# A graph attention layer on one core: the factor of neighbour j moves from h into the weights, the mask becomes a minimum, and h is split in chunk 0 by ScalarE and VectorE

## What is computed

```
h  = relu(layernorm(x)) @ W1 + b1                      # 4096 x 256
e  = leaky_relu((h @ a1)[:, None] + (h @ a2)[None, :] + b2, 0.2)
attention = softmax(where(adj > 0, e, -1e12), axis=1)  # row i over neighbours j
out = x + elu(attention @ h)
```

## Time and profile before

| what | value |
|---|---|
| median of 3 runs | 459.96 us |
| lowest and highest run | 459.87, 460.02 us |
| span of the profiled execution | 458.2 us (its own time isn't shown) |
| median less span | 1.76 us |
| busy share of the span: TensorE, VectorE, ScalarE, POOL | 93%, 85%, 67%, 28% |
| mean granted TensorE clock | 0.989 |
| DMA | 80.60 MB, mean 176 GB/s |

### The profile page before, as it was taken

The page is one execution under the profiler, slowest core; times in us unless marked ns, Lnnn a source line. Parts: engine busy times, 40 slices in busy tenths (PEclk is TensorE's granted clock), DMA queues, the critical chain, the costliest instruction groups (busy, mean ns, idle before and its releaser), DMA issues.

```text
span 458.2 us, 8873 instructions
## 1 busy us (share of the span) xinstructions
PE 423.9 (93%) x3399; PEld 416.1 (91%) x3399; DVE 387.6 (85%) x388; ACT 309.1 (67%) x297; POOL 126.3 (28%) x155
## 2 busy tenths in 40 slices
PE   0799879788889999999999999999999999999995
PEld 0789879787888899999999999999999999999995
DVE  3999799999998805999999549999996399999915
ACT  2687898777665418995776289958663789586603
POOL 3242289999999940000000000000000000000004
PEclk9999998989899999999999999999999999999999
DMA  8930025554543630754738806656468156566202
GB/s 279 382 132 1 1 92 185 183 185 185 183 176 109 240 118 14 263 199 169 255 158 285 292 21 226 232 183 224 188 237 295 63 191 259 192 208 250 92 0 92
DMA packets 22355, 80.60 MB, mean 176 GB/s; under 512 B 1472, under 2 KB 14016, under 8 KB 14144
## 3 DMA queue, kind: packets, MB, share of 16 engines
q1 hardware_dynamic: 21920, 79.70, 49.0%
q10 hardware_dynamic: 416, 0.66, 0.4%
HBM read 76.15 MB, written 4.19 MB: 175 GB/s over the span
## 4 chain that ended last, share of the span: by engine, by line
PE 67%; POOL 12%; issue 9%; DVE 7%; DMA 2%; POOLq 1%; ACT 1%; SPq 0%; DVEq 0%; ACTq 0%
PE ps L599 39%; PE ps L601 19%; POOL h_raw L325 12%; DVE stats L656 2%; DMA x_s<-x 2%; PE ps L617 1%; PE ps L616 1%; PE ps L615 1%; DVE hnT_lo L683 1%; PE ps L526 1%; DVE h_raw L692 1%; PE ps L528 1%; PE ps L527 1%; DVE y L868 1%; DVE xn L673 1%
## 5 line engine op out<-in xcount | busy, mean ns | idle before, releaser
L599 PE MATMUL ps<-hp_hi,w_hi 128*128 (+1 forms) x960 | 240.5, 288 | 12.7 <-POOL hp_lo L328 12.5
L601 PE MATMUL ps<-hp_lo,w_hi 128*128 (+1 forms) x960 | 238.1, 285 | 0.0
L730 DVE SCALAR_TENSOR_TENSOR adj_s<-R,p,adj_s 128x1024 f32<-128x1024 f32 x128 | 171.7, 1382 | 38.8 <-ACT adj_s L392 38.8
L599 PEld LDWEIGHTS ps<-hp_hi,w_hi 128*128 128x128 f32 x960 | 184.5, 192 | 17.4 <-issue 12.7
L601 PEld LDWEIGHTS ps<-hp_lo,w_hi 128*128 128x128 f32 x960 | 184.4, 192 | 0.0
L400 ACT ACTIVATE w_hi<-adj_s 128x2048 fp32r<-128x2048 f32 x64 | 122.5, 1913 | 56.0 <-DVE adj_s L730 38.5
L740 DVE SCALAR_TENSOR_TENSOR w_lo<-adj_s,w_hi 128x2048 fp32r<-128x2048 f32 x64 | 153.1, 2394 | 3.7 <-ACT w_hi L400 3.7
L392 ACT ACTIVATE adj_s<-adj_s 128x2048 f32<-128x2048 int32 x64 | 122.2, 1910 | 20.1 <-DMA adj_s<-adj_t 20.1
L599 PE MATMUL ps<-hp_hi,w_lo 128*128 (+1 forms) x960 | 125.2, 283 | 0.6 <-DVE w_lo L740 0.6
L599 PEld LDWEIGHTS ps<-hp_hi,w_lo 128*128 128x128 f32 x960 | 119.5, 189 | 0.8 <-DVE w_lo L740 0.8
L339 POOL TENSOR_TENSOR adj_s<-y,adj_s 128x256 f32<-128x256 f32 x8 | 5.7, 712 | 283.8 <-DVE y L868 283.5
(11 more groups left out here) (88 smaller groups left out, 269.1 us busy)
## 6 DMA issues: line engine op xcount, KB each, us to landing
adj_s<-adj_t SPq DMA_DIRECT2D x64, 1024.0 KB, 4.8
x_s<-x SPq DMA_DIRECT2D x8, 512.0 KB, 10.4
o_s<-x SPq DMA_DIRECT2D x3, 1024.0 KB, 8.5
out<-o_s SPq DMA_DIRECT2D x6, 512.0 KB, 6.9
adj_s<-x SPq DMA_DIRECT2D x1, 1024.0 KB, 5.5
out<-adj_s SPq DMA_DIRECT2D x8, 128.0 KB, 1.7
vec<-vectors ACTq DMA_DIRECT2D x1, 384.5 KB, 6.4
W1x<-W ACTq DMA_DIRECT2D x1, 256.0 KB, 4.4
```

The source lines that it names most:

```text
L599: last = pe.matmul(acc, block_w, hh, start=False, stop=False)
L601: pe.matmul(acc, block_w, hl, start=False, stop=False)
L730: last = dve.scalar_tensor_tensor(sgn, R[:, ds(ic * CW, CW)], p[:, ds(source(r, c) + s, 1)], sgn, ALU.max, ALU.mult)
```

## The change

The factor u_j is taken out of h and put into the weight:

- `sign` (the name stays) is a Relu with the factor 2^102, so that it gives 0 or a very large number; the mask is a minimum with it.
- `high` is a copy with the factor u of each tile, so two instructions of 1024 columns in place of one of 2048; `low` likewise is two instructions, weight times u less `w_hi`. `high` of the first pair leaves group 7 and comes in its place in the loop, after u.
- `hp_hi` is now the rounded h (`round_h`, a pair in one instruction), and `hp_lo` is h less `hp_hi` (`low_h`, a pair in one instruction on VectorE). POOL's loop is gone.
- TensorE waits for `hp_ready` once a pair, and multiplies with 256 columns of `hp_lo`, since the low part of the columns 1 and 0 is zero. The other matmuls keep 258.

```diff
+BIG = 2.0 ** 102
@@ gpsimd
-            def hp_low(jb):
-                rows = h_raw[:, ds(jb, 1), :]
-                pool.wait_ge(hp_tile, jb + 1)
-                pool.tensor_tensor(rows, rows, u[:, ds(jb, 1)].unsqueeze(2).broadcast_to([P, 1, HW]), ALU.mult)\
-                    .then_inc(hp_whole, 1)
-                pool.wait_ge(hp_whole, jb - 1)
-                pool.tensor_tensor(hp_lo[:, ds(jb, 1), :], rows, hp_hi[:, ds(jb, 1), :].bitcast(fp32), ALU.subtract)\
-                    .then_inc(hp_ready, 1)
-            with pool.Fori(2, TILES) as jb:
-                hp_low(jb)
@@ scalar
-                act.activation(adj_w[:, c, :, :], adj_s[:, c, :, :], ACT.Sign).then_inc(signed, 1)
+                act.activation(adj_w[:, c, :, :], adj_s[:, c, :, :], ACT.Relu, scale=BIG).then_inc(signed, 1)
...
-                act.activation(w_hi[:, c, :, :], adj_w[:, c, :, :], ACT.Relu).then_inc(hi_ready, 1)
+                for s in range(2):
+                    last = act.activation(w_hi[:, c, s, :], adj_w[:, c, s, :], ACT.Copy, scale=u[:, ds(source(r, c) + s, 1)])
+                last.then_inc(hi_ready, 1)
...
-                if g == 7:
-                    high(0, 0, 0)
...
+            def round_h(r, c):
+                pair = ds(source(r, c), 2)
+                act.activation(hp_hi[:, pair, :], h_raw[:, pair, :], ACT.Copy).then_inc(hp_pair, 1)
+            act.wait_ge(ones_col, 1)
+            round_h(0, 0)
             act.wait_ge(g_ready, 1)
             act.activation(u[:, :], s2[:, :], ACT.Exp, bias=gm[:, 4:5]).then_inc(u_ready, 1)
-            def hp_high(r, c):
-                for s in range(2):
-                    jb = source(r, c) + s
-                    act.activation(hp_hi[:, ds(jb, 1), :], h_raw[:, ds(jb, 1), :], ACT.Copy,
-                                   scale=u[:, ds(jb, 1)]).then_inc(hp_tile, 1)
@@ scalar, round_of
-                        hp_high(*ahead(ic, r, c, 1)[1:])
+                        round_h(*ahead(ic, r, c, 1)[1:])
...
-                    if not (first and r is FIRST_ROUND and c == 0):
-                        high(ic, r, c)
+                    high(ic, r, c)
...
-            act.wait_ge(ones_col, 1)
             act.wait_ge(u_ready, 1)
-            hp_high(0, 0)
             keep_s(GROUPS - 2)
@@ tensor, pair
-                        if first and part == 0:
-                            if begin:
-                                pe.wait_ge(hp_first, s + 1)
-                            else:
-                                pe.wait_ge(hp_ready, 2 * m + s - 1)
+                        if first and part == 0 and s == 0:
+                            pe.wait_ge(hp_ready, m + 1)
...
-                        hl = hp_lo[:, ds(2 * m + s, 1), :]
+                        hl = hp_lo[:, ds(2 * m + s, 1), 0:F]
...
-                                pe.matmul(acc, block_w, hl, start=False, stop=False)
+                                pe.matmul(ps[:, ib, 0:F].unsqueeze(1), block_w, hl, start=False, stop=False)
@@ vector
-                                                    ALU.max, ALU.mult)
+                                                    ALU.max, ALU.min)
...
-                dve.scalar_tensor_tensor(w_lo[:, c, :, :], adj_w[:, c, :, :], 0.0, w_hi[:, c, :, :].bitcast(fp32),
-                                         ALU.max, ALU.subtract).then_inc(lo_ready, 1)
+                for s in range(2):
+                    last = dve.scalar_tensor_tensor(w_lo[:, c, s, :], adj_w[:, c, s, :], u[:, ds(source(r, c) + s, 1)],
+                                                    w_hi[:, c, s, :].bitcast(fp32), ALU.mult, ALU.subtract)
+                last.then_inc(lo_ready, 1)
...
+            def low_h(r, c):
+                pair = ds(source(r, c), 2)
+                dve.wait_ge(hp_pair, pair_no(0, r, c) + 1)
+                dve.tensor_tensor(hp_lo[:, pair, :], h_raw[:, pair, :], hp_hi[:, pair, :].bitcast(fp32), ALU.subtract)\
+                    .then_inc(hp_ready, 1)
@@ vector, round_of
                     low(ic, r, c)
+                    if first and not (r is LAST_ROUND and c == SLOTS - 1):
+                        low_h(*ahead(ic, r, c, 1)[1:])
...
-            for jb in range(2):
-                dve.wait_ge(hp_tile, jb + 1)
-                dve.scalar_tensor_tensor(hp_lo[:, jb, :], h_raw[:, jb, :], u[:, jb:jb + 1], hp_hi[:, jb, :].bitcast(fp32),
-                                         ALU.mult, ALU.subtract).then_inc(hp_first, 1)
+            low_h(0, 0)
             dve.wait_ge(p_ready, 2)
+            dve.wait_ge(u_ready, 1)
```

More of the change, by code:

```diff
@@ L197, in build @@
         eps_ready = sem("eps_ready")
-        hp_tile = sem("hp_tile")
         dve_y = sem("dve_y")
         dve_o = sem("dve_o")
-        hp_first = sem("hp_first")
-        hp_whole = sem("hp_whole")
+        hp_pair = sem("hp_pair")
         hp_ready = sem("hp_ready")
@@ L607, in last_pair @@
                 if first:
-                    pe.wait_ge(hp_ready, 2 * m)
+                    pe.wait_ge(hp_ready, m + 1)
                 for ib in range(BANKS):
@@ L613, in last_pair @@
                         hh = hp_hi[:, ds(2 * m + s, 1), :]
-                        hl = hp_lo[:, ds(2 * m + s, 1), :]
+                        hl = hp_lo[:, ds(2 * m + s, 1), 0:F]
                         pe.matmul(acc, w_hi[:, b, s, col], hh, start=False, stop=False)
-                        pe.matmul(acc, w_hi[:, b, s, col], hl, start=False, stop=False)
+                        pe.matmul(ps[:, ib, 0:F].unsqueeze(1), w_hi[:, b, s, col], hl, start=False, stop=False)
                         last = pe.matmul(acc, w_lo[:, b, s, col], hh, start=False, stop=s == 1)
```

## The result

The changed kernel takes **440.53 us** (median of 4 runs, 439.96 to 440.69), the kernel before 459.91 beside it (459.67 to 460.02). The ratio is 0.9578, 95% interval 0.9565 to 0.9592: faster by 4.2%. The forecast was 440.5. The profiled execution is the fastest of the four: 439.96 us at a span of 438.2; the spans of the four are 438.2, 438.6, 438.9 and 438.9.

The account below looks back on a forecast made before the run. TensorE bounds the later chunks, POOL's split of h chunk 0 (24.1 us excess). With +3.1 us at the start, 1.7 for the clock and 0.2 saved on columns, the span goes from 458.2 to 438.8, the median to 440.5 us; range 437.6 to 446.0.

Parts of the forecast that it names:

- What bounded chunk 0: Chunk 0: POOL's multiply and subtract, 6.9 us a pair against TensorE's 5.75, hold it back; excess 24.1 us.
- `low` and `high` in two: Every pair: `low` +0.18 us on VectorE, `high` +0.3 on ScalarE, both hidden; `low` with 5 us to spare in chunk 2.
- The start: Before chunk 0: weights of pair 0 need u, so the first main matmul moves from 57.69 to 60.8, +3.1 us.
- The clock: Behind the 3 us gap at the start: TensorE falls to half clock once, losing 1.7 us.
- The two columns: 1024 matmuls stream 256 columns, not 258: 0.2 us saved in all; bounds nothing and 0.95.
- The sum: Chunk 0 ends at 154.8, not 174.05; less 0.2 for columns, span 438.8, median 440.5 us; chance 0.60.
- C: Last pair of a chunk: VectorE's lead runs out before it, at a cycle over 5.13 us; 443 to 455 us, chance 0.14.
- D: Whole loop: VectorE becomes the bound, each half of `low` costing 1.684 us, cycle 5.76; 471 us, chance 0.04.
- B: Gap at the start: the clock doesn't fall there; 438.8 us, chance 0.20.

Follow-up runs that it names:

- dve_little: The changed kernel with one more VectorE instruction of 200 columns behind `low` of every pair, 0.28 us a pair; 440.59 us.
- dve_more: The changed kernel with one more VectorE instruction of 488 columns behind `low` of every pair, 0.58 us a pair; 454.68 us.
- high_first: The changed kernel with `high` of the very first pair ahead of the two `keep_s` and `round_h` of the next pair on ScalarE; 437.27 us.
- cols258: The changed kernel with `hp_lo` multiplied with 258 columns again, all else the same; 440.73 us.
- u_in_h_halves: u_in_h_dve with `low` of the very first pair in two instructions of 1024 columns, TensorE waiting for each; 437.00 us.
- fill18: The changed kernel with twelve more restarts ahead of the six, in the gap before the first main matmul; 438.65 us.
- pool_subtracts: The changed kernel with POOL subtracting, one instruction a tile for tiles 2 to 31, and VectorE without `low_h` after the first pair; 440.44 us.
- start_split: The changed kernel with `high` of pair 0 by halves around the `keep_s`, TensorE waiting for each half, and six more restarts; 437.58 us.
- u_in_h_dve: The kernel before with u still in h, but VectorE writing `hp_lo` of all tiles and POOL's loop gone; 436.87 us.

## Why the prediction was right

- **What bounded chunk 0.** The 24.1 us of excess were POOL's, as the step has it: chunk 0 falls to 93.16 us when VectorE splits h with the factor left where it was, and the changed kernel's time stays when POOL keeps one of its two instructions a tile.
- **`low` and `high` in two.** +0.18 us and +0.3 us a pair were forecast; `low` measured 2.39 us for two (start to start), `high` 60.48 - 58.40 = 2.08. Both are hidden in every chunk: `w_lo` of chunk 2's last pair is ready at 329.4 and wanted at 334.4, the 5 us of the forecast. dve_little and dve_more bracket the margin: there are between 0.28 and 0.58 us a pair left. The forecast put the limit at a cycle of 5.13, 0.35 above the kernel's.
- **The start.** +3.1 forecast, 60.62 - 57.69 = 2.9 measured; high_first shows that ScalarE's order sets it.
- **The clock.** Once, 1.7 us forecast; 1.4 to 1.5 measured in the profiled execution. The size and the count were right; the cause is only in part what the step said, that the gap of 3 us brings the clock down. Here it stood at 0.50 at 57.0, ahead of the gap, after the thin work from 54 us on, over which the kernel before kept 1.00.

  The moment differs between executions of nearly the same start: in cols258, whose row follows, the clock fell at 60.1, inside the gap, in dve_little at 58.2. And it fell at 57.0 in u_in_h_halves too, which has no gap. What the gap does show is how long the fall lasts: there the clock was back at 60.4, in the changed kernel, idle until 60.62, at 63.8. That the clock also fell in the three executions of the changed kernel that weren't profiled is likely (mean clock 0.990 or 0.991, but the mean takes in the tail too, where the clock is at half again from 435.9 us on), not shown.

  By the rule of the Trainium skill, "TensorE: Matmul & The Clock Gate", section "What's actually happening", activity releases the throttle; these two traces agree, with the clock at 1.00 only after TensorE had been at work again (60.4 and 63.8). fill18 doesn't test it, since its clock never fell there.

```profile
60.00:61.00 1.00, 0.35 (x1) 0.35 (x2) 0.37 (x1) 1.00 (x2) 0.00 (x0) 0.53 0.00 0
```

- **The two columns.** 0.2 forecast, 0.36 measured, under the 0.85 and the 0.95 that the prediction set beside it.
- **The sum.** Chunk 0 ended at 154.34, forecast 154.8; the span is 438.2, forecast 438.8. In the profiled execution the small errors don't cancel: the start came 0.2 us sooner, the clock cost 0.3 less and the columns saved 0.15 more in the later chunks than forecast, 0.6 us together. That the median, 440.53, meets the forecast to 0.03 us is luck: it lies 0.6 us above the profiled execution, and what the slower ones spent isn't traced. The clock is a candidate. It was at half until 64.2 in pool_subtracts and 65.0 in dve_little, and their chunk 0 took 93.89 and 94.18 us, against 93.72 here.

The rivals C and D didn't occur, though both are real: C is what dve_more shows, and D's price is nearly there as soon as POOL works beside VectorE, 1.64 us for a half of `low` in pool_subtracts. B didn't occur here, but did in high_first and fill18, both of which change the start.

What the forecast didn't ask is whether the change's parts belong together. Only one earns much. Moving the split to VectorE is worth 23 us (459.7 to 436.9). Moving the factor into the weight costs 3.7 (436.87 against 440.53; 3.9 against cols258, which ran beside it with the same 258 columns): the start, the fall of the clock there, and nothing back but the 0.4 us of the columns, since VectorE can do both of POOL's operations in one instruction with the factor where it was. The fastest kernel by the median is the one with u left in h, 436.87 us; high_first, start_split and u_in_h_halves come within 0.8 us of it.

## What to carry to other kernels

Before a factor is moved to take work off a slow engine, try the same work on the engine with room, in one fused instruction; and ask what the moved operand now depends on, since the first tile's chain gets longer by it. An engine's cycle below the bound's is not enough where a lead is lost at every chunk and wanted in full at its end: compute when the last item is ready, not only the rate. An idle stretch ahead of the main loop can cost twice, by itself and by TensorE's clock in the stretch behind it: 2.9 and 1.4 us here.

## What was not expected

- The clock at the start differs between executions of one program, by the times and the mean clocks: high_first took 437.1 to 437.3 us at a mean clock of 1.0 and 439.0 to 439.7 at 0.99; u_in_h_dve 436.8 to 436.9 (0.997 to 0.999) and 437.5 to 437.7 (0.993 to 0.996).
- VectorE beside POOL: with POOL's subtraction of 258 columns alone, halves of `low` take 1.642 us on the mean of chunk 0 instead of 1.278, and masks 1.334 instead of 1.277.
